# Attention value products per block of tokens: transposed probabilities stationary, values moving

## The reference

```python
h = layernorm(x) * (1 + ca) + sa
q, k, v = (einsum('bnd,ed->bne', h, W) for W in (Wq, Wk, Wv))   # (b, 512, 16*64), split into heads
q, k = l2norm(q) * q_scale, l2norm(k) * k_scale
attn = softmax(einsum('bhid,bhjd->bhij', q, k) * 64 ** -0.5)
out = einsum('bhij,bhjd->bhid', attn, v)                        # the value products
x = x + ga * (out.reshape(b, n, 1024) @ Wo.T + bo)
```

## Time and profile before

| | us |
|---|---|
| median of 3 runs | 1406.56 |
| lowest and highest run | 1404.82 and 1412.9 |
| profiled execution, its own time | 1406.78 |
| its span, first to last instruction | 1405.0 |
| attention (50 us to 1060 us of the span), PE busy | 958.45 of 1010 |
| attention, DVE, ACT and POOL busy | 812.43, 708.29 and 670.33 of 1010 |

### The profile page before, as it was taken

How to read it: one execution, slowest core, us unless ns; L and a number is a source line. 1 busy time by engine, 2 the same in 40 slices (tenths; PEclk the granted TensorE clock), 3 DMA queues, 4 the chain that set the end, 5 groups by cost and what they waited for, 6 DMA issues and landing times. The chain is left out here.

```text
span 1405.0 us, 31811 instructions
## 1 busy us (share of the span) xinstructions
PE 1262.1 (90%) x9674; PEld 828.6 (59%) x9674; DVE 1107.3 (79%) x1995; ACT 952.9 (68%) x2014; POOL 858.0 (61%) x1659
## 2 busy tenths in 40 slices
PE   4899999989999999999899999999994477899997
PEld 4555565656555565556566555666552355677775
DVE  3778878878878887788788788877873996788887
ACT  3677677767666776677677766777762565777776
POOL 2577666766666776666667667676754664444443
PEclk8899999999999999999999999999998699999999
DMA  5000000000000000000000000000002000535341
GB/s 131 2 2 1 2 1 2 2 4 2 1 4 2 2 2 4 2 2 2 4 1 2 3 2 2 2 1 2 2 1 75 1 0 9 131 86 104 89 89 38
DMA packets 53202, 28.60 MB, mean 20 GB/s; under 512 B 8720, under 2 KB 51224, under 8 KB 53016
## 3 DMA queue, kind: packets, MB, share of 16 engines
q1 hardware_dynamic: 51832, 25.99, 7.7%
q10 hardware_dynamic: 1184, 0.40, 0.1%
HBM read 24.16 MB, written 2.23 MB: 19 GB/s over the span
## 5 line engine op out<-in xcount | busy, mean ns | idle before, releaser
L697 ACT ACTIVATE probs<-bank,neg_max 128x512 f32<-128x512 f32 x512 | 347.5, 684 | 280.3 <-DVE neg_max L815 259.5
L815 DVE TENSOR_REDUCE neg_max<-bank 128x1 f32<-128x512 f32 x512 | 329.3, 685 | 165.4 <-PE bank L516 162.0
L556 PE MATMUL bank<-probsT,qkv 128*64 128x512 f32 x1024 | 280.7, 628 | 0.9 <-DVE oT L832 0.9
L516 PE MATMUL bank<-operands 64*128 64x512 f32 x1536 | 255.9, 439 | 0.9 <-DVE operands L810 0.5
L993 POOL TENSOR_TENSOR inv_wide<-inv_sum,consts 128x512 f32<-128x512 f32 x64 | 66.5, 1039 | 237.7 <-DVE inv_sum L826 237.7
L532 PEld LDWEIGHTS T<-ident,probs 64*128 64x128 f32 x4096 | 173.6, 142 | 40.3 <-issue 10.2
L532 PE MATMUL T<-ident,probs 64*128 64x64 f32 x4096 | 173.6, 226 | 1.5 <-issue 0.7
L486 PEld LDWEIGHTS bank<-operands,hT_h 128*128 128x128 f32 x254 | 48.2, 190 | 213.0 <-issue 209.4
L516 PEld LDWEIGHTS bank<-operands 64*128 64x128 f32 x1536 | 128.4, 190 | 63.5 <-issue 44.2
L1627 POOL TENSOR_TENSOR hid_l<-gated,hid_h 128x512 fp32r<-128x512 f32 x64 | 89.4, 1397 | 123.3 <-ACT hid_h L1544 123.3
L977 POOL TENSOR_TENSOR sq<-qkv 128x256 f32<-128x256 f32 x252 | 150.9, 615 | 11.9 <-ACT qkv L676 9.7
(11 more groups left out here) (235 smaller groups left out, 2399.7 us busy)
## 6 DMA issues: line engine op xcount, KB each, us to landing
probsT<-gate_scratch SPq DMA_DIRECT2D x64, 256.0 KB, 4.9
out<-x_all SPq DMA_DIRECT2D x8, 256.0 KB, 2.3
probsT<-in_L_ffn_fc_w SPq DMA_DIRECT2D x1, 1024.0 KB, 9.4
raw<-in_L_attn_Wq SPq DMA_DIRECT2D x1, 512.0 KB, 4.4
raw<-in_L_attn_Wk SPq DMA_DIRECT2D x1, 512.0 KB, 7.3
raw<-in_L_attn_Wv SPq DMA_DIRECT2D x1, 512.0 KB, 8.6
raw_o<-in_L_attn_Wo SPq DMA_DIRECT2D x1, 512.0 KB, 8.7
probsT<-in_L_ffn_sh_w SPq DMA_DIRECT2D x2, 256.0 KB, 2.7
```

Of the source, the lines that this page charges most:

```text
L516: last = nc.tensor.matmul(s_bank(hp, 2 * pair + head)[:], own[rows, q, toks], own[rows, k], start=((q, k) == (QH, KH)), stop=(q == QL))
L556: last = nc.tensor.matmul(O_BANK[rows, :], qkv[:, hp % 4, j, cols], probsT[:, hp % 2, head, j], start=(j == 0), stop=(j == NT - 1), skip_g ...
L697: nc.scalar.activation(probs[:, i % 4], s_bank(hp, i)[:], ACT.Exp, bias=neg_max[:, i:i + 1], accum_out=row_sum[:, hp % 2, i:i + 1]).then_i ...
L815: nc.vector.reduce_max(neg_max[:, i:i + 1], s_bank(hp, i)[:], AX.X, negate=True).then_inc(max_done, 1)
```

## The change

Each value product now has a 128 x 128 block of transposed probabilities stationary and the 128 x 64 block of v moving. `weigh_values(w, hp, t)` makes a block t of 128 query tokens complete: 2 heads by 4 key blocks, 8 matmuls of 64 columns, in place of 2 of 512. It stands ahead of the quarter's scores, and the four quarters of one slot make one unit. The output is tokens by channels, so the inverse sums apply per row (`normalise` reads them directly), and widening, transposing and copying them falls away. The result is transposed on PE (`transpose_out`, in quarter 1, in the place of `inverse_rows`), and ACT and DVE split it from PSUM (`high_o`, `low_o`) in place of POOL's `split_o`. `normalise` moves from quarter 2 to the start of quarter 0. `probsT` is kept once, by query block, in place of twice. `split_h1` moves from DVE to POOL, and `ln_rows` uses another instruction with the same result.

```diff
                 for t in range(NT):
-                    last = nc.vector.tensor_scalar(h_ln[:, t], tile_of(b, t), mean_var[:, t, 0:1], rstd[:, t:t + 1],
-                                                   ALU.subtract, ALU.mult)
+                    last = nc.vector.scalar_tensor_tensor(out=h_ln[:, t], in0=tile_of(b, t), scalar=mean_var[:, t, 0:1],
+                                                          in1=rstd[:, t:t + 1].to_broadcast([P, C]), op0=ALU.subtract,
+                                                          op1=ALU.mult)
...
-                    def inverse_rows(u, *free):
-
-                        pe.wait_ge(wide_done, u + 1)
+                    def transpose_out(w, *free):
+
+                        pe.wait_ge(o_done, w + 1)
                         for semaphore, value in free:
                             after(pe, semaphore, value)
                         for t in range(NT):
-                            last = nc.tensor.transpose(XT_BANK[:, t * P:(t + 1) * P],
-                                                       inv_wide[:, t].rearrange("p h d -> p (h d)"), ident[:])
-                        last.then_inc(r_ready, 1)
-
-                    def weigh_values(u, hp, j):
-
-                        if j == 0:
-                            pe.wait_ge(t_dve, 2 * (u + 1))
-                            pe.wait_ge(t_act, 2 * (u + 1))
-                            after(pe, o_done, u)
+                            last = nc.tensor.transpose(XT_BANK[:, t * P:(t + 1) * P], o_tok[:, t], ident[:])
+                        last.then_inc(ot_ready, 1)
+
+                    def weigh_values(w, hp, t):
+
+                        copied, count = ((t_dve, 1), (t_act, 1), (t_dve, 2), (t_act, 2))[t]
+                        pe.wait_ge(copied, 2 * w + count)
+                        if t == 0:
+                            after(pe, o_done, w)
                         for head in range(2):
-                            rows = slice(head * DH, (head + 1) * DH)
+                            at = (2 * t + head) * DH
                             cols = slice(2 * P + head * DH, 2 * P + (head + 1) * DH)
-                            last = nc.tensor.matmul(O_BANK[rows, :], qkv[:, hp % 4, j, cols],
-                                                    probsT[:, hp % 2, head, j], start=(j == 0), stop=(j == NT - 1),
-                                                    skip_group_check=True)
-                        last.then_inc(av_step, 1)
+                            for j in range(NT):
+                                last = nc.tensor.matmul(O_BANK[:, at:at + DH], by_pair[:, t, head, j], qkv[:, hp % 4, j, cols],
+                                                        start=(j == 0), stop=(j == NT - 1))
+                        last.then_inc(av_done, 1)
...
-                            if pair == 1 and earlier >= 1:
-                                inverse_rows(u - 1, side)
-                                side = (r_copied, u)
+                            if pair == 1 and earlier >= 2:
+                                transpose_out(u - 2, side)
+                                side = (ol_done, u - 1)
                             if main and pair == 2 and with_next(b, hp, 1):
                                 transpose_q(u + 1, hp + 1, side)
                             if main and pair == 3 and with_next(b, hp, 1):
                                 transpose_k(u + 1, hp + 1)
+                            if earlier >= 1:
+                                weigh_values(u - 1, hp - 1, pair)
                             if main:
                                 scores(u, hp, pair)
                             if pair < 2 and earlier >= 1:
                                 transpose_probs(u - 1, pair + 2)
                             if pair >= 2 and main:
                                 transpose_probs(u, pair - 2)
-                            if pair < 2 and earlier >= 2:
-                                weigh_values(u - 2, hp - 2, pair + 2)
-                            if pair >= 2 and earlier >= 1:
-                                weigh_values(u - 1, hp - 1, pair - 2)
...
-                    def normalise(u, hp):
-                        dve.wait_ge(av_step, NT * (u + 1))
-                        dve.wait_ge(r_copied, u + 1)
-                        after(dve, ol_done, u)
-                        nc.vector.tensor_tensor(oT[:], O_BANK[:], inv_row[:, hp % 2], ALU.mult).then_inc(o_done, 1)
+                    def normalise(w, hp):
+                        dve.wait_ge(av_done, NT * (w + 1))
+                        dve.wait_ge(inv_done, w + 1)
+                        after(dve, ot_ready, w)
+                        by = inv_sum[:, hp % 2].unsqueeze(2).to_broadcast([P, S_TILES, DH])
+                        nc.vector.tensor_tensor(o_tok[:].rearrange("p t (h d) -> p (t h) d", h=2),
+                                                O_BANK[:].rearrange("p (k d) -> p k d", d=DH), by, ALU.mult).then_inc(o_done, 1)
+
+                    def low_o(w, hp):
+                        dve.wait_ge(oh_done, w + 1)
+                        nc.vector.tensor_tensor(oT_l[:, hp % HP], XT_BANK[:], oT_h[:, hp % HP].bitcast(F32),
+                                                ALU.subtract).then_inc(ol_done, 1)
...
-                            if pair == 2 and earlier >= 2:
+                            if pair == 0 and earlier >= 2:
                                 normalise(u - 2, hp - 2)
...
+                            if pair == 1 and earlier >= 2:
+                                low_o(u - 2, hp - 2)
```

More of the change, by code:

```diff
@@ L400, in adaln_attention_moe @@
             inv_done = sem("inv_done")
[L401 to L404, removed]
+            av_done = sem("av_done")
             o_done = sem("o_done")
+            ot_ready = sem("ot_ready")
             oh_done = sem("oh_done")
@@ L662, in _ @@
                     slot(B, 0, main=False)
-                    for j in (2, 3):
-                        weigh_values(HP * B - 1, HP - 1, j)
-                    project_out(LAST, 3, (r_copied, HP * B), (y_more, 3 * LAST + 2))
+                    transpose_out(HP * B - 1, (ol_done, HP * B - 1))
+                    project_out(LAST, 3, (y_more, 3 * LAST + 2))
                     transpose_y(LAST)
@@ L674, in copy_projection @@
                         act.wait_ge(pj_ready, NT * w + t + 1)
-                        after(act, av_step, NT * (w - 4) + t + 1)
+                        after(act, av_done, NT * (w - 3))
                         nc.scalar.activation(qkv[:, hp % 4, t], bank[:, 0:3 * P], ACT.Copy).then_inc(pj_copied, 1)
@@ L701, in copy_transposed, with high_o @@
                         act.wait_ge(t_ready, NT * u + pair + 1)
-                        nc.scalar.activation(pair_tiles(hp, pair), t_pair, ACT.Copy).then_inc(t_act, 1)
-                    def copy_inverse(u, hp):
-                        act.wait_ge(r_ready, u + 1)
-                        after(act, o_done, u - 1)
-                        nc.scalar.activation(inv_row[:, hp % 2], XT_BANK[:], ACT.Copy).then_inc(r_copied, 1)
+                        after(act, av_done, NT * (u - 1) + pair + 1)
+                        nc.scalar.activation(pair_tiles(pair), t_pair, ACT.Copy).then_inc(t_act, 1)
+                    def high_o(w, hp):
+                        act.wait_ge(ot_ready, w + 1)
+                        nc.scalar.activation(oT_h[:, hp % HP], XT_BANK[:], ACT.Copy).then_inc(oh_done, 1)
                     def modulate1(b):
@@ L744, in slot @@
                                     modulate2(b - 1)
-                            if pair == 1 and earlier >= 1:
-                                copy_inverse(u - 1, hp - 1)
+                            if pair == 1 and earlier >= 2:
+                                high_o(u - 2, hp - 2)
                             if main and pair == 2 and with_next(b, hp, 1):
@@ L838, in take_mod @@
                         last.then_inc(done, 1)
-                    def split_h1(b, t):
-                        dve.wait_ge(h1_done, b + 1)
-                        after(dve, pj_ready, NT * (HP * b - 1) + t + 1)
-                        toks = slice(t * P, (t + 1) * P)
-                        nc.vector.tensor_copy(hT_h[:, toks], h1_out[:, toks]).then_inc(h1h_done, 1)
-                        dve.wait_ge(h1h_done, NT * b + t + 1)
-                        nc.vector.tensor_tensor(hT_l[:, toks], h1_out[:, toks], hT_h[:, toks].bitcast(F32),
-                                                ALU.subtract).then_inc(hT_ready, 1)
                     def add_y(b, k):
@@ L897, in norm_first @@
                             ln_rows(dve, *rows)
-                        if not is_const(b, LAST) and (hp, pair) in ((5, 1), (5, 2), (5, 3), (6, 0)):
-                            split_h1(b + 1, (pair - 1) % NT)
                     def norm_last(b, hp, pair):
@@ L946, in _ @@
                     take_mod(mod1, (CA, SA), 0, mod1_done, (h1_done, 0))
-                    for t in range(NT):
```

(16 more changed lines are left out.)

42 lines of the change are left out of this document (16 added, 26 removed).

## The result

The changed kernel takes 1750.53 us (median of 4 runs, 1742.98 to 1757.2) against 1409.73 (1404.82 to 1413.94) for the kernel before on the same chip: 1.2417 times the time, with a 95% interval of 1.2345 to 1.249. It is slower, as forecast; the time is 36 us under the 1786 us forecast and inside the range of 1640 to 1910. Its profiled execution took 1752.95 us, that of before 1406.78; the 346.2 us between these two are what has to be accounted for.

What follows compares the result with a forecast made beforehand. PE's own work was taken to bound the kernel, so additions are paid in full: 1406.8 + 235 (value blocks) + 192 (waits) + 4 (`normalise`) - 52 (layer norms) = 1786 us, with a range of 1640 to 1910 us.

Steps and rivals of the forecast that it cites:

- PE has no slack, so what is added is paid: PE's own work sets the pace in attention; work added to a quarter is paid in full, 256 times.
- The value block: Value products on PE: 16 loads at the router's pace make a block 1.93 us, not 1.01; +235 us over 256 blocks.
- The order on PE: Value products ahead of scores uncover DVE's chain: 1.07 us waits in quarters 2, 3 and 0, 61 slots, +192 us.
- `normalise` in quarter 0: A slot's first value block waits for `normalise`, 0.1 to 0.6 us on some 30 slots: +4 us.
- Layer norms: PE's stalls at `ln_rows` go because quarter 3 begins later: 4.1 us each, 14 times, -52 us in all.
- I take it as hidden: At `ln_rows`, at most 0.5 us of PE's wait left, 14 times, 7 us upper cost; counted as nothing.
- Start and end: Start and end of the kernel, where DVE's and POOL's splits move to other engines: nothing, within 5 us.
- the clock falls: Rival: PE's clock halves again and again in attention, half the quarters at +1.0 us, +128, 1914 us; chance 0.14.

Runs made afterwards that it cites:

- kernel 2: Changed kernel with each value product split into two halves of 64 query tokens, side by side on the output partitions: 1567.68 us, 1.1104 of before.
- kernel 1: Changed kernel with the value products back behind the quarter's probability transposes on PE: 1541.08 us, 1.0929 of before.
- 7: Kernel before with its own value products, in their old form, moved ahead of the scores: 1594.28 us, 1.1315 of before.
- 5: Changed kernel with `low_o` ahead of the two row maxima of quarter 1 on DVE: 1698.69 us, 1.2071 of before.
- kernel 3: Changed kernel with `ln_rows` using the old `tensor_scalar` again: 1751.69 us, 1.2424 of before.
- kernel 6: Changed kernel with value products both behind the probability transposes and split into two halves of 64 query tokens: 1397.83 us, 0.9919 of before.
- kernel 4: Kernel before with only `ln_rows` changed to the new instruction, `scalar_tensor_tensor`: 1412.58 us, 1.0011 of before.
- kernel 8: Kernel before with POOL held in the slots of hp 0 and hp 3 until `ln_rows` is done: 1418.09 us, 1.0055 of before.

## Why the prediction was right, and where it was off

- **PE has no slack, so what is added is paid.** Right: the other engines have less work and none of it shows.
- **The value block.** The mechanism was right (kernel 2: the width of the loads bounds it) and so was the load's pace, 0.111 us as forecast. The size was off, and this is the term that failed: "Eight loads more give 0.99 + 8 x 0.111 = 1.88 us", plus 0.053, "the block grows by 0.92 us, 256 times: +235 us". Quarter 1, which has no wait, grew from 3.55 to 4.28 us, by 0.73, so the term is 187 us. What failed is the overlap at the block's start. From its first load to the next group's first load (782.62 to 784.55) the block is 1.93 us, just as forecast; but the forecast's other terms go from product to product, and the first load begins 0.11 us ahead of the first product, under the transposes. From product to product the block is 1.82. The transposes themselves, 0.53 us before, cost 0.44 (782.29 to 782.73), with the block behind them in place of the scores; in kernel 1, where the scores follow them, they are at 0.53 again. The two make the 0.2 us.
- **The order on PE.** Right in mechanism, places and price. Kernels 1 and 7 isolate it and 5 takes out one of the three. From start to start of the projections (line 486, now 485), in the median, quarter 2 grew from 3.56 to 5.32 us, quarter 3 from 3.65 to 5.38, and quarter 0 with an output projection from 4.60 to 6.33. Less 0.73 each, that leaves waits of 1.03, 1.00 and 1.00 us, 3.03 a slot against 3.14. Over 61 slots it is 185 us, against 192.
- **`normalise` in quarter 0.** Forecast +4, and right within 3 us, though the waits do not list it. Where the side task is four transposes, the block follows `normalise` (line 827) by 0.15 us each time:

```profile
777.55 0.68 DVE L827 TENSOR_TENSOR o_tok<-bank,inv_sum 128x512 f32<-128x512 f32 x1
...
778.37 1.97 PE L555 MATMUL bank<-qkv,probsT 128*128 128x64 f32 x16
```

  Behind such transposes it starts after 0.60 us, where it does after 0.46 in quarters 2 and 3, and costs 1.90 in place of 1.83. That is 0.2 us in 21 slots; with 0.1 in the router's and 0.36 in the five that have no side task the term is about 7 us. The 8.8 us listed ahead of line 555 are 6 waits in slots without transposes there: four in batch 0, two in batch 7.
- **Layer norms.** The stall went, as forecast, and the term is 52 us by the lengths of these quarters. But the reason given was incomplete. It named the longer quarters alone, by which at most 0.5 us of a wait would be left "even if the new instruction is no faster". In fact the four instructions take 1.18 us, since POOL hardly works beside them any more (0.416 us each in the mean, and 0.348 for 48 of the old form in kernel 3), and behind them DVE has 1.21 us to spare until the next scores:

```profile
796.26 1.29 DVE L811 TENSOR_REDUCE neg_max<-bank 128x1 f32<-128x512 f32 x2 [1.21 <-PE bank L515]
```

  At 3.39 us for four they would have overrun that by 1.0 us, twice the forecast's bound, an estimate from these rows. So "I take it as hidden" was right in part by luck. In kernel 6, with quarters of 3.63 us and 2.2 us for four, 18.5 us of waits are back.
- **Start and end.** "I leave at nothing, within 5 us" was wrong. The end of attention grew by 32.2 us, of which its 16 blocks at 0.73 are 11.7 and the waits of the 61st slot 3.0; 17.5 are over, and the start has 1.5 and the rest of the kernel 0.5. The clock is halved for a part of it:

```profile
1367.16 1.09 PE L501 MATMUL bank<-ident,qkv 128*128 128x128 f32 x4 [1.28 <-DVE operands L799]
1368.04 3.52 PE L555 MATMUL bank<-qkv,probsT 128*128 128x64 f32 x16
1371.48 1.65 PE L515 MATMUL bank<-operands 64*128 64x512 f32 x6
```

  and by windows:

```profile
1367.90:1371.40 3.50, 3.50 (x18) 3.46 (x16) 0.24 (x1) 0.60 (x1) 0.00 (x0) 0.50 0.00 0
```

  The last slots have no projections and PE waits 1.28 us here, after 1.58 and 1.57 us at 1350.30 and 1360.34; the block costs 3.44 us at the clock of 0.50, the level of 1.2 GHz. The seven blocks that ran wholly or in part at that level took 21.8 us by their rows, where seven at 1.83 are 12.8: 9 us of the 17.5. The rival "the clock falls" holds in the last slots, not in the body; had it come true in the body, it would have cost more than its 1914 us, since it took the block as unchanged by the clock.
- **Sum.** Against the terms of the forecast the blocks are -48, the waits -7, `normalise` +3, start, end and the rest +19.5, and the holes at the jumps, which it did not have, +3. Another -3 are waits that the kernel before already had: in twelve slots its quarter 2 took 3.8 to 3.9 us in place of 3.56. Together that is -32.5, where 1786 and the profiled 1753 are 33 apart. The total came nearer than its largest term because errors of 48 and 19.5 us had opposite signs, which is luck.

## What to carry to other kernels

Swapping the stationary and the moving operand changes what bounds a matmul: count the loads, and where a stationary block is used once for few columns, its price is the load's pace, which narrower blocks on separate output partitions can lower. On an engine that is never idle, each piece of work also covers somebody's latency, so moving it costs what it covered; before moving it, find the chain that ends just as it ends. And say for each term by which rows it is measured, loads or products: lengths of both kinds do not add up end to end. Last, time the parts of a change apart: this one loses 24% as written, and gains 0.8% with two small edits.

## What the runs showed of the hardware

- **Blocks bound by loads slow down with the clock.** At a granted clock of 0.50 the block of sixteen loads costs 3.44 us, at 1.00 it costs 1.83. The page "TensorE: Matmul & The Clock Gate" of the Trainium skill (LDWEIGHTS) gives a load's time by its columns alone; at the full clock the trace's pace of 0.111 us is near the 107 ns that it gives for 128 columns (an estimate by its formula), at half the clock the measurement decides otherwise.
- **64 columns of weights, two abreast, in 0.0675 us a pair.** Kernel 2's block of 16 such pairs costs 1.08 us, where 16 loads of 128 columns take 1.82.
- **DVE beside POOL.** Four 128 x 128 f32 instructions of DVE in SBUF take 3.1 to 3.6 us beside POOL's work in the kernel before, and 3.40 in the other form (kernel 4); the old form takes 0.34 us each with POOL held (kernel 8).
- **The jump back of a loop.** PE's hole there is 1.8 to 1.9 us before, whose last block is 4 long records, and 3.7 to 4.4 us in kernel 6, whose last block is 32 short ones. But it is 1.6 to 1.9 us in kernel 1 too, whose last block is 16 short records. What sets it was not tried by itself.
